# Four attention layers in a loop over the batch: GpSimd sums six key tiles instead of five, and steps of TensorE change places

## What is computed

```python
# layer 0: 8 heads of 32 channels over the 1024 places
attn = softmax(einsum('bihd,bjhd->bijh', q, k) * 32**-0.5, axis=2)
x = einsum('bijh,bjhd->bihd', attn, v) @ w_out + b_out + x
# layer 1: group norm (32 groups), one head of 256 channels
x = x + wo @ attention(wq @ gn(x), wk @ gn(x), wv @ gn(x)) + bo
# layer 2: mean-std norm for queries and keys, one head of 256 channels
x = x + ow @ (h(x) @ softmax(f(norm(x)).T @ g(norm(x))).T) + ob
# layer 3: mixture of softmaxes, keys softmaxed over 16 channels, pooled queries and values,
# then w_out, batch norm over all 8 images, + x
```

## Time and profile before

| | us |
|---|---|
| median of 3 runs | 2934.55 (2933.15 to 2943.73) |
| profiled execution | 2939.64 |
| its span, first to last instruction | 2937.9 |
| TensorE busy | 2644.1 |
| VectorE busy | 1995.7 |
| ScalarE busy | 1289.3 |
| GpSimd busy | 698.1 |

### The profile page before, as it was taken

The page is one execution under the profiler, slowest core; times in us unless marked ns, Lnnn a source line. Parts: engine busy times, 40 slices in busy tenths (PEclk is TensorE's granted clock), DMA queues, the critical chain, the costliest instruction groups (busy, mean ns, idle before and its releaser), DMA issues.

```text
span 2937.9 us, 43959 instructions
## 1 busy us (share of the span) xinstructions
PE 2644.1 (90%) x15676; PEld 1846.5 (63%) x15676; DVE 1995.7 (68%) x2297; ACT 1289.3 (44%) x1874; POOL 698.1 (24%) x444
## 2 busy tenths in 40 slices
PE   5898999899898998989989899898999999898994
PEld 4457765477655775557755677456775577655772
DVE  3665786666876767766776677775776666866666
ACT  2463335534354433644346343463435533355334
POOL 0440035300361013600236002450025300352001
PEclk7899999999999999999989999999999999999997
DMA  5200022000410004000150002300023000320007
GB/s 129 62 16 1 12 65 73 16 1 11 101 37 16 1 11 108 30 16 1 32 116 2 16 12 57 80 2 16 12 61 76 16 1 12 76 62 1 1 25 301
DMA packets 46237, 123.51 MB, mean 42 GB/s; under 512 B 9904, under 2 KB 21424, under 8 KB 42416
## 3 DMA queue, kind: packets, MB, share of 16 engines
q1 hardware_dynamic: 46000, 120.36, 15.3%
HBM read 41.96 MB, written 23.86 MB: 22 GB/s over the span
## 4 chain that ended last, share of the span: by engine, by line
PE 70%; issue 11%; DVE 6%; ACT 4%; SPq 4%; POOL 3%; DMA 1%; ACTq 0%; DVEq 0%; POOLq 0%
PE tile L1533 22%; PE pv L1533 11%; PE pv L1657 8%; PE tile L1619 7%; PE tile L1647 5%; PE tile L1780 4%; PE tile L1681 4%; SPq L576 3%; PE pv L1647 2%; PE tile L1802 2%; PE tile L1831 2%; DMA stack<-qk_r 1%; ACT p L848 1%; POOL qk_r L681 1%; PE tile L1709 1%
## 5 line engine op out<-in xcount | busy, mean ns | idle before, releaser
L1118 DVE TENSOR_REDUCE small<-tile 128x1 f32<-128x1024 f32 x512 | 603.6, 1218 | 199.7 <-PE tile L1619 197.5
L848 ACT ACTIVATE p<-tile 128x512 f32<-128x512 f32 (+1 forms) x632 | 405.6, 690 | 271.2 <-PE tile L1647 234.1
L1619 PE MATMUL tile<-stack 96*128 96x512 f32 x1024 | 375.1, 463 | 26.9 <-DMA stack<-qk_r 15.1
L739 POOL TENSOR_TENSOR row_sum<-act 128x256 f32<-128x256 f32 x32 | 41.6, 1318 | 1503.0 <-DVE act L1311 1503.0
L1533 PE MATMUL tile<-qk_r 128*128 128x512 f32 x1536 | 378.0, 395 | 0.0
L709 POOL TENSOR_TENSOR acc<-acc,p 128x1024 f32<-128x1024 f32 x144 | 339.1, 2383 | 19.5 <-ACT p L848 19.5
L1533 PEld LDWEIGHTS tile<-qk_r 128*128 128x128 f32 x1536 | 287.3, 188 | 66.4 <-issue 7.7
L1619 PEld LDWEIGHTS tile<-stack 96*128 96x128 f32 x1024 | 189.9, 205 | 205.3 <-issue 124.3
L1316 DVE TENSOR_TENSOR pl<-p,ph 128x1024 fp32r<-128x1024 f32 x128 | 158.2, 1236 | 221.0 <-ACT p L930 221.0
L1647 PE MATMUL tile<-stack 112*128 112x512 f32 x760 | 277.7, 433 | 28.5 <-ACT p L848 28.3
L1657 PE MATMUL pv<-p,v 128*32 128x512 f32 x2048 | 278.2, 617 | 1.4 <-ACT p L848 1.4
(11 more groups left out here) (282 smaller groups left out, 4451.3 us busy)
## 6 DMA issues: line engine op xcount, KB each, us to landing
stack<-qk_r SPq DMA_DIRECT2D x192, 256.0 KB, 5.0
x_in<-in_x_dram SPq DMA_DIRECT2D x8, 1024.0 KB, 5.0
act<-in_x_dram SPq DMA_DIRECT2D x8, 1024.0 KB, 5.5
x_scratch<-act SPq DMA_DIRECT2D x7, 1024.0 KB, 4.0
z_scratch<-act SPq DMA_DIRECT2D x7, 1024.0 KB, 3.9
stack<-ones SPq DMA_DIRECT2D x16, 256.0 KB, 4.7
w3f<-w3f_scratch SPq DMA_DIRECT2D x8, 512.0 KB, 3.3
fin_rest<-z_scratch SPq DMA_DIRECT2D x3, 1024.0 KB, 9.6
```

The lines of the kernel that those rows point to most:

```text
L848: sc.activation(p0[:, jt % DEPTH, pair, first:first + len(heads) * HALF], tile_wait(batch, "st0", *u, jt, k), ACT.Exp, scale=float(D) ** - ...
L1118: ve.tensor_reduce(maxima[:, h * NT + it:h * NT + it + 1], t, X, ALU.max).then_inc(vector_done, vector.one("max0", g, h, it))
L1619: ins = mm(o[:, s], stack[0:IMAX, g, 0, h, it * P:(it + 1) * P], stack[0:IMAX, g, 1, h, s], start=True, stop=True)
```

## The change

1. SUMMED goes from 5 to 6: GpSimd adds ten times in place of eight in the units (0,0), (0,1) and (1,0), and den0 of these has three tile groups in place of four.
2. GpSimd makes the residue of the former unit behind the additions of a unit, not after the second tile's.
3. In the last unit den0 comes ahead of the value groups of tiles 6 and 7, with the sum ahead of tile 7.
4. In the key stage both smt tiles stand at k = 4, all of qk0(1,1) at k = 6, the halves of z at k = 8, 10, 12 and 14. ScalarE's list has smt_kept(0) ahead of g_kept, and qk0(1,1)'s parts ahead of z_kept(0). VectorE sums the second half's windows right behind qv_in, takes the logits at k = 2 and the rest of the mixing at k = 3.
5. TensorE does group norm's averages, the projections of layer 1 and v(1,0) at the end of the former turn, ahead of the jump; of_projections puts them into the step lists' head part. The places of tiles in PSUM change for eight tiles of the key stage alone.

```diff
-SUMMED = 5
+SUMMED = 6
...
@@ tensor_steps @@
-        s += {1: [("mt",)], 2: [("qk0", 0, 1), ("g",)], 4: [("smt", 0)], 5: [("smt", 1)], 9: [("z", 0)], 11: [("qk0", 1, 1)],
+        s += {1: [("mt",)], 2: [("qk0", 0, 1), ("g",)], 4: [("smt", 0), ("smt", 1)], 6: [("qk0", 1, 1)], 10: [("z", 0)],
               14: [("z", 1)]}.get(k, [])
...
@@ scalar_steps @@
-    s += [("mix_exp",), ("g_kept", 0), ("g_kept", 1), ("smt_kept", 0), ("smt_kept", 1)]
-    s += [("z_kept", 0), ("qk0_hi", 1, 1), ("qk0_full", 1), ("z_kept", 1)]
+    s += [("mix_exp",), ("smt_kept", 0), ("g_kept", 0), ("g_kept", 1), ("smt_kept", 1)]
+    s += [("qk0_hi", 1, 1), ("qk0_full", 1), ("z_kept", 0), ("z_kept", 1)]
...
@@ vector_steps @@
-    s += [("win_max", 1), ("kt_sub", 1), ("win_sum", 0), ("win_rec", 0), ("qv_in",)]
+    s += [("win_max", 1), ("kt_sub", 1), ("win_sum", 0), ("win_rec", 0), ("qv_in",), ("win_sum", 1), ("win_rec", 1)]
     for k in range(G * HT):
-        s += [("win_sum", 1), ("win_rec", 1), ("mt_in",), ("kbar",), ("sm", 1)] if k == 1 else []
-        s += [("mix", n) for n in range(4)] + [("mix_sum",), ("mix_rec",), ("mix_pi",)] if k == 3 else []
+        s += {1: [("mt_in",), ("kbar",), ("sm", 1)], 2: [("mix", n) for n in range(4)],
+              3: [("mix_sum",), ("mix_rec",), ("mix_pi",)]}.get(k, [])
...
@@ gpsimd, turn, in the loop over the units @@
-                        if jt == 2 and last_unit(*u):
-                            g, half = last_unit(*u)
...
+                    if last_unit(*u):
+                        g, half = last_unit(*u)
+                        cols_ = slice(half * HALF, (half + 1) * HALF)
+                        pool.wait_ge(scalar_done, scalar.at(b, "res_hi", g, half))
+                        pe.tensor_tensor(side[:, 1, g, cols_], raw[:, cols_], side[:, 0, g, cols_].bitcast(F32),
+                                         ALU.subtract).then_inc(pool_done, gps.one("res_lo", g, half))
...
@@ tensor, den0 @@
-                    for jt in (*range(top, NT), top - 1):
+                    order = (*range(top, NT), top - 1) if next_unit(g, half) else (*range(top, NT - 1), top - 1, NT - 1)
+                    for jt in order:
...
@@ tensor, turn @@
-                for layer in (1, 2) if not first else ():
-                    if layer == 1:
-                        vector_wait("mv", 1, 1)
...
+                for layer in (1, 2) if not first else ():
+                    if layer == 2:
+                        vector_wait("feat_lo", 2, 0, CT - 1)
+                        v_tile(2, 0)
+                        if not last:
+                            v0_tile(0)
+                            v0_tile(1)
+                        qk_tiles(2)
...
-                    if body and k in (4, 5):
-                        smt_tile(k - 4)
-                    if body and k in (7, 9, 12, 14):
-                        z_half(*((0, 0), (0, 1), (1, 0), (1, 1))[(7, 9, 12, 14).index(k)])
-                    if head and k in (10, 11):
-                        qk0(1, 1, (k - 10,))
+                    if body and k == 4:
+                        smt_tile(0)
+                        smt_tile(1)
+                    if head and k == 6:
+                        qk0(1, 1)
+                    if body and k in (8, 10, 12, 14):
+                        z_half(*divmod(k // 2 - 4, 2))
...
+                        if not following and jt == NT - 1:
+                            den0(*u)
                         if jt:
                             pv0(*u, jt - 1)
...
+                    pv0(*u, NT - 1)
                     if following:
-                        pv0(*u, NT - 1)
                         m0(*following)
                         den0(*u)
-                    else:
-                        den0(*u)
-                        pv0(*u, NT - 1)
                 if head:
                     ex0(*UNITS[-1])
                     out0(1)
+                    group_norm()
+                    qk_tiles(1)
+                    v_tile(1, 0)
```

More of the change, by code:

```diff
@@ L109, in tensor_steps @@
     for layer in (1, 2):
-        s += [("gn",), ("pv_groups",)] if layer == 1 else [("v", 2, 0), ("v0", 0), ("v0", 1)]
-        s += [("qk", layer, t, ct) for t in range(2) for ct in range(CT)]
-        s += [("v", 1, 0)] if layer == 1 else []
+        s += [("v", 2, 0), ("v0", 0), ("v0", 1)] + [("qk", 2, t, ct) for t in range(2) for ct in range(CT)] if layer == 2 else []
         s += [("s", layer, it) for it in range(NT)] + [("v", layer, 1)]
@@ L129, in tensor_steps @@
                 s += [("st0", *u, jt, k)] if kind == "st0" else [("s0", *rows_of(next_unit(*u), 2 * jt + k))]
+            s += [("den0", *u)] if not next_unit(*u) and jt == NT - 1 else []
             s += [("pv0", *u, jt - 1)] if jt else []
@@ L132, in tensor_steps @@
             s += [("out0", 0)] if u == UNITS[-1] and jt == 4 else []
-        s += [("pv0", *u, NT - 1), ("m0", *next_unit(*u)), ("den0", *u)] if next_unit(*u) else (
-            [("den0", *u), ("pv0", *u, NT - 1)])
+        s += [("pv0", *u, NT - 1)] + ([("m0", *next_unit(*u)), ("den0", *u)] if next_unit(*u) else [])
     s += [("ex0", *UNITS[-1]), ("out0", 1)]
-    return s
+    return s + [("gn",), ("pv_groups",)] + [("qk", 1, t, ct) for t in range(2) for ct in range(CT)] + [("v", 1, 0)]
 def scalar_steps():
@@ L991, in turn @@
                 if body:
+                    z_kept(0)
                     z_kept(1)
@@ L1681, in den0 @@
                                 ins = mm(o[D * h:D * h + D, 0:P], seg, src[:, h // 2, i:i + P],
-                                         start=t == 0 and jt == top, stop=t == HT - 1 and jt == top - 1)
+                                         start=t == 0 and jt == order[0], stop=t == HT - 1 and jt == order[-1])
                     ins.then_inc(tensor_done, tensor.one("den0", g, half))
@@ new lines, in group_norm @@
+                def group_norm():
+                    vector_wait("mv", 1, 1)
+                    o = free("gn")
+                    mm(o[:, 0:2], gn_avg[:], mv[:, :, 0], start=True, stop=True)
+                    mm(o[:, 2:4], gn_rest[:], mv[:, :, 0], start=True, stop=True)
+                    mm(o[:, 4:6], gn_avg[:], mv[:, :, 1], start=True, stop=False
+                       ).then_inc(tensor_done, tensor.one("gn"))
+                    vector_wait("gn")
+                    mm(o[:, 4:6], gn_avg[:], gsq, start=False, stop=True
+                       ).then_inc(tensor_done, tensor.one("pv_groups"))
@@ new lines, in v_tile @@
+                def v_tile(layer, k):
+                    if layer == 2 and k == 1:
+                        vector_wait("feat_lo", 2, 1, CT - 1)
+                    feat = (xh, xl) if layer == 1 else (side[:, 0], side[:, 1])
+                    wh, wl = wqk[layer, "v", "h"], wqk[layer, "v", "l"]
+                    o = free("v", layer, k)
+                    for q in range(4):
+                        j = slice((4 * k + q) * P, (4 * k + q + 1) * P)
+                        ins = three(o[:, q * C:(q + 1) * C], [[v[:, kt_, j] for kt_ in kts] for v in feat],
+                                    [[w[:, kt_, :] for kt_ in kts] for w in (wh, wl)])
+                    ins.then_inc(tensor_done, tensor.one("v", layer, k))
@@ L1759, in turn, with qk_tiles @@
+                def qk_tiles(layer):
                     for t in range(2):
```

50 lines of the change are left out of this document (11 added, 39 removed).

## The result

The changed kernel takes 2973.96 us (median of 4 runs, 2971.85 to 2975.13) where the kernel before takes 2935.32 beside it (4 runs, 2933.15 to 2943.73): a ratio of 1.0125 with a 95% interval of 1.0105 to 1.0146: slower by 1.25%, clear of the noise. The profiled execution has a span of 2971.4 us.

The account below looks back on a forecast made before the run. TensorE, busy 90% of the span, bounds the kernel through its work and idle time. Sums +83, last unit -7.7, keys -33.6, mixing -5, edge 0 gave +37 on the median 2934.55: 2972 us, range 2862 to 2996.

Parts of the forecast that it names:

- The additions: GpSimd in a unit: ten additions from 4.6 to 28.1 us, the residue behind them ending at 29.4.
- The turn: Negate on VectorE: its operations wait one GpSimd addition apart, so TensorE's m0 starts 2.25 to 3.5 us late.
- the 8.05 of the sum: TensorE's holes at m0 in a batch's three units: 2.25, 2.9 and 2.9 us.
- the other case: First rival, at negate: tensor_scalar and copy do not wait, TensorE sees nothing; -68 us, 2866; chance 0.33.
- The clock: TensorE behind each hole: a low granted clock loses 1.7 us, bounds 0 and 1.7.
- the DMA stop: Key stage: TensorE's stop behind the stack's DMAs and its clock tail go, 4.2 x 8 = -33.6 us.
- The mixing's 0.75 us: Key stage's mixing chain: earlier maximum 0.6 and smt(1) 0.15 us, 0.75 x 7 = -5; bounds -20 and +5.
- The last unit's -7.7: Last unit: earlier denominators remove TensorE's wait for the rows before ex0, -7.7 us; bounds -7.7 and 0.
- The edge's 0: Loop edge: old stop after the jump goes, a new one may come at s(1,0); 0 us, bounds -10 and +20.
- +83: Sixth summed tile over eight batches: holes and clock tails less the removed denominator matmuls, +10.4 us a batch.
- -46: Gains outside the sums: last unit -7.7, key stage's DMA stop -33.6, mixing -5 us.
- its likeliest case: The forecast that negate waits behind GpSimd, chance 0.55; alone it spans 2950 to 3002 us.

Follow-up runs that it names:

- the run without holes: Changed kernel with GpSimd's tenth addition waiting for negate's last operation, and the loop's edge of the kernel before: 2869.47 us, ratio 0.9765.
- GpSimd's own pause: Changed kernel with GpSimd waiting, ahead of its tenth addition, for the end of its own ninth only: 2916.71 us, ratio 0.9908.
- the kernel with the wait: Changed kernel with GpSimd's tenth addition issued only after negate's last operation has ended: 2870.99 us, ratio 0.9764.

## Why the prediction was right, and which step was not

The sign and the cause came out as forecast: negate late behind GpSimd's additions, 24 times, with a low clock behind 22 of the 24 holes. The time, 2974 against 2972, is nearer than the terms are, and that is luck (see the sum below).

**The additions.** Ten from 4.6 to 28.1 and the residue to 29.4, said the prediction; counted from the unit's first matmul at 1196.24 they run from 4.6 to 28.0 and 29.3.

**The turn.** The step that failed is "if the tensor_scalar or the copy ahead of it waits too, they come one addition apart: the first runs at 25.75, addition ten goes next because it is queued, and the copy and the last operation come behind it at 28.3". In the changed kernel no turns were taken. The scaling alone waited, through both boundaries, and the other two came free behind it: 4.27 us and twice 0.17 instead of three waits. The case that the prediction counted on, the residue slipping in between copy and last operation, gave nearly the right end for the wrong reason: the residue was waited for by the scaling, as one more part of the run. That is why the holes are near: 2.4, 3.2 and 3.3 us more idle time than with five sums or before (31.71 - 28.00 against 29.27 - 27.94 with five sums; 34.52 - 30.87 against 30.59 - 30.16; 34.41 - 30.68 against 30.61 - 30.17), 8.9 against the 8.05 of the sum. The first number comes from this stretch of the kernel with five sums:

```profile
1132.23:1161.50 29.27, 27.94 (x132) 14.55 (x132) 23.14 (x25) 18.18 (x36) 18.82 (x8) 0.88 0.37 99
```

**Its reason.** The prediction took the wait from the pace of a tensor_scalar and counted the other case, where only a two-input operation waits, at 0.33. The runs show that the scaling and a two-input operation in its place are held alike (4.27 and 4.26 us), so the pace was not what mattered, while bn_stats beside the same additions keeps its 683 ns (684 before). The earlier trace rows had shown a wait for one GpSimd operation with nothing queued behind it, which can't tell an instruction from a run. The Trainium skill (SBUF — State Buffer, section Who interferes with whom) lets a tensor_scalar in its two-port mode and an operation with two SBUF inputs contend with GpSimd, with the second comer blocked for the whole instruction of the first; the trace agrees on who contends, and on how long it differs: 4.27 us is more than the 2.35 of one addition, and 8.85 more than three.

**The clock.** 1.7 us a hole was taken. The second unit's TensorE is busy 30.87 us where it was 30.16 with 0.91 us more work: 1.6. Over the run, the 87 us of the sixth tile, with the 21.8 us of removed matmuls added and the 69 us of holes taken off, leave 40 us, 1.7 a hole if all of it is the clock's. So the size was right on average; its reading was not, since 0.66 is a third of the way from 0.5 to 1, not halfway (5 us at 0.66 do lose 1.7). The holes are not alike: behind two of the first batch (2.42 us each) the granted clock stayed at 1.00, behind three others (3.3 us) it was 0.90 over the next 30 us, a loss of 3 us and beyond the bound of 1.7.

**Keys, last unit, edge.** The change without its sixth tile is 55 us faster than the kernel before (2887.40 against 2942.41); these three terms of the sum made 46. The largest share is in the first unit, 4.67 us (33.94 to 29.27), against 4.2 taken for the DMA stop. The mixing's 0.75 us is 0.9 in the one turn looked at: TensorE's timeline has a stop of 1.94 us at an s0 tile in place of 2.84 at smt(1):

```profile
1139.44 1.55 PE L1625 MATMUL tile<-stack 96*128 96x512 f32 x4 [1.94 <-DVE small L1120]
```

The last unit's -7.7 is not decided: its wait came back (7.7 us) with the old order, the time by 4 us in runs that overlap. The edge's 0 agrees with the run without holes; with holes, a cost of 5.6 us is hinted at and not shown.

**The sum.** +83 was 87 and -46 was -55: +32 in place of +37, against the kernel before at 2942. Beside the changed kernel it ran at 2935, which makes +39; those 7 us are the spread of the kernel before itself. That the forecast met the result within 2 us is luck within this spread. The prediction's range ended at 2996, below the 3002 that it gave its likeliest case; the result tests neither. The terms were near for the change as a whole, but they can't be undone one by one: the six sums cost 54 us alone and 87 beside the rest, the key stage's return costs 25 beside six sums where its two terms made 39, because hole and stop share the first unit.

## What to carry to other kernels

An operation of VectorE that reads and writes SBUF alone may be held not for one GpSimd instruction but until GpSimd's run of back-to-back work is over. That is the worst case seen here and not a rule: behind GpSimd's own pause the hold was one addition. If it stands on the path that sets the end, count to the end of the run, or break the run with a wait on that very operation. One wait of two lines turned a change that lost 1.25% into one that gains 2.35%. And a stop removed next to a new one should be priced with both present: the six sums cost 54 us without the other parts of the change and 87 with them.

## What the runs showed of the hardware that was not expected

- A 0.17 us VectorE operation was held for up to 4.35 us with ten additions in GpSimd's run, about as long in the two-input form (4.26 us in the unit shown), and for up to 8.96 us with twelve. A GpSimd pause of some 0.1 us let it in.
- The other way round no such hold was seen. In the last unit, amid VectorE's own additions, GpSimd's residue of 1.26 us took 2.23: it waited for the rest of one addition and got in. VectorE's and GpSimd's timelines there, in the kernel with the wait:

```profile
1222.55 2.35 DVE L1154 TENSOR_TENSOR acc<-p 128x1024 f32<-128x1024 f32 x2
1224.82 5.71 DVE L1154 TENSOR_TENSOR acc<-acc,p 128x1024 f32<-128x1024 f32 x4
...
1224.95 2.23 POOL L720 TENSOR_TENSOR side<-raw,side 128x512 fp32r<-128x512 f32 x1 [5.72 <-ACT side L874]
```

- Holes of nearly the same length cost TensorE's clock or don't. In the kernel with GpSimd's own pause, two holes ahead of the last unit of two batches have 1.89 and 1.87 us; over the 30 us behind the longer one the granted clock is 1.00, behind the shorter one 0.94. The two rows of m0:

```profile
536.78 0.60 PE L1637 MATMUL tile<-ident,small 128*16 128x128 f32 x4 [1.89 <-DVE small L1133]
888.64 0.87 PE L1637 MATMUL tile<-ident,small 128*16 128x128 f32 x4 [1.87 <-DVE small L1133]
```

The stretches behind them, columns as in the earlier trace rows:

```profile
536.78:566.78 30.00, 29.68 (x315) 16.41 (x316) 20.64 (x22) 18.55 (x23) 4.35 (x3) 1.00 0.06 15
888.64:918.64 30.00, 29.73 (x310) 16.58 (x311) 19.73 (x21) 17.92 (x22) 4.35 (x3) 0.94 0.01 2
```
